# Four-layer attention kernel: in the fourth layer the softmax rows are scaled by ScalarE instead of VectorE, and the normed tokens are transposed as two ring jobs

## What is computed

```python
h = _mamba2_block(x, ...)                       # state-space scan over 112 steps, 8 heads of 64
xn = _ln(h, ln_w, ln_b)
q = (xn @ Wq).reshape(b, Lq, N_HEADS, dh)       # k = enc @ Wk, v = enc @ Wv the same way
scores = jnp.einsum('bqhd,bkhd->bhqk', q, k) * np.float32(1.0 / np.sqrt(dh))
scores = jnp.where(pad_mask[:, None, None, :], jnp.float32(-1000000000.0), scores)
p = jax.nn.softmax(scores, axis=-1)
ctx = jnp.einsum('bhqk,bkhd->bqhd', p, v).reshape(b, Lq, D)
return h + ctx @ Wo
```

## Time and profile before

| | |
|---|---|
| median of three runs | 3705.43 us (3703.78 to 3712.94) |
| profiled execution, its own time | 3712.93 us |
| its span in the trace | 3711.1 us |
| TensorE, VectorE, ScalarE, GpSimd busy | 93%, 52%, 50%, 11% |
| mean granted TensorE clock | 0.966 of full speed |
| fourth layer's attention and state turns | 3169 to 3711 us of the span |

### The profile page before, as it was taken

How to read it: one execution, slowest core, us unless ns; L and a number is a source line. 1 busy time by engine, 2 the same in 40 slices (tenths; PEclk the granted TensorE clock), 3 DMA queues, 4 the chain that set the end, 5 groups by cost and what they waited for, 6 DMA issues and landing times. The chain is left out here.

```text
span 3711.1 us, 67817 instructions
## 1 busy us (share of the span) xinstructions
PE 3461.5 (93%) x21748; PEld 2540.5 (68%) x21748; DVE 1933.5 (52%) x5863; ACT 1853.4 (50%) x5421; POOL 404.5 (11%) x488
## 2 busy tenths in 40 slices
PE   8999999999988999999979999999999997888888
PEld 6778778778866666666656766667667664555665
DVE  3654644654544444444544544544554545566656
ACT  3543544544445555555545555545545552444444
POOL 2101101101101111111010000000000001112111
PEclk9999999999998999999989999999999997898999
DMA  6000000000004000000010000000000000000000
GB/s 204 4 12 15 4 12 15 4 12 15 4 21 131 14 13 13 13 8 5 13 53 8 9 8 15 9 8 15 8 8 14 9 3 14 22 16 13 13 26 5
DMA packets 58462, 75.11 MB, mean 20 GB/s; under 512 B 6752, under 2 KB 55584, under 8 KB 57024
## 3 DMA queue, kind: packets, MB, share of 16 engines
q1 hardware_dynamic: 58176, 71.45, 6.3%
HBM read 64.04 MB, written 7.40 MB: 19 GB/s over the span
## 5 line engine op out<-in xcount | busy, mean ns | idle before, releaser
L161 PE MATMUL l_bank<-l_xT,weights_of_layers_and 128*128 128x224 f32 x2816 | 622.0, 374 | 18.7 <-ACT l_xT L1137 8.0
L161 PEld LDWEIGHTS l_bank<-l_xT,weights_of_layers_and 128*128 128x128 f32 x2816 | 546.4, 201 | 65.6 <-ACT l_xT L1137 8.7
L387 ACT ACTIVATE l_pT<-l_bank 125x336 f32<-125x336 f32 (+2 forms) x736 | 347.0, 471 | 339.5 <-PE l_bank L319 329.2
L319 PEld LDWEIGHTS l_bank<-identity,l_p 112*125 112x125 f32 (+2 forms) x2336 | 334.8, 178 | 185.6 <-issue 98.1
L319 PE MATMUL l_bank<-identity,l_p 112*125 112x112 f32 (+2 forms) x2336 | 390.1, 279 | 22.8 <-DVE l_p L363 18.5
L404 ACT ACTIVATE l_p<-l_p,l_nm 112x375 f32<-112x375 f32 x384 | 233.4, 608 | 287.2 <-DVE l_nm L438 285.9
L161 PE MATMUL l_bank<-weights_of_layers_and,l_cT 128*125 128x256 f32 (+2 forms) x960 | 303.3, 454 | 11.4 <-DVE l_queries_or_hidden L1839 9.3
L161 PE MATMUL l_bank<-l_cT,weights_of_layers_and 128*128 128x375 f32 x832 | 305.6, 497 | 0.0
L704 POOL TENSOR_TENSOR l_ve<-l_mv,eps 112x2 f32<-112x2 f32 (+1 forms) x89 | 17.3, 195 | 2434.7 <-DVE l_mv L698 2434.7
L363 DVE TENSOR_SCALAR l_p<-l_p,l_rs 112x375 f32<-112x375 f32 (+1 forms) x608 | 256.4, 422 | 21.7
L400 ACT ACTIVATE l_p<-l_p,l_nm 112x112 f32<-112x112 f32 x512 | 192.2, 377 | 150.7 <-DVE l_nm L434 131.9
(11 more groups left out here) (252 smaller groups left out, 5790.3 us busy)
## 6 DMA issues: line engine op xcount, KB each, us to landing
l_cT<-in_ctx_turned SPq DMA_DIRECT2D x32, 375.0 KB, 3.5
l_cx<-in_ctx SPq DMA_DIRECT2D x16, 375.0 KB
context_rows<-in_ctx_reversed SPq DMA_DIRECT2D x16, 375.0 KB
tokens<-x_after_layer SPq DMA_DIRECT2D x25, 224.0 KB, 2.6
x_after_layer<-l_z SPq DMA_DIRECT2D x24, 224.0 KB, 2.4
weights_of_layers_and<-bias_lines_kept SPq DMA_DIRECT2D x1, 2625.0 KB, 16.2
weights_of_layers_and<-in_L_xattn_w_fused SPq DMA_DIRECT2D x1, 2048.0 KB, 10.9
weights_of_layers_and<-in_L_xattn_w_ff SPq DMA_DIRECT2D x1, 2048.0 KB, 12.9
```

Source lines behind the costliest of these rows:

```text
L161: last = pe.matmul(out, left, right, start=(k == 0), stop=(k == len(pairs) - 1))
L319: last = pe.transpose(TR.bank(m)[:ph.keys, g * ph.rows:(g + 1) * ph.rows], p[:ph.rows, m % self.p_slots, g * ph.keys:(g + 1) * ph.keys], i ...
L387: return act.activation(out, src, ACT.Copy)
```

## The change

1. The cross attention's `Part` gets `scaled_by="act"`. The multiplication of an item's probabilities by the reciprocal moves from VectorE (a tensor_scalar) to ScalarE (an activation Copy whose scale is the column `rs`), in place as before. On ScalarE it stands in step n for item n-1, behind the exponential of item n. VectorE keeps the reciprocal. 128 instructions move. The other layers' parts keep their engines.
2. The job `yT` becomes two jobs, `yT0` and `yT1`, of 224 columns each in a bank of its own. ScalarE copies each as soon as it is there. `cq` waits for `yT1`. The ring's list has 33 jobs now.

```diff
3678.60:3711.10 32.50, Columns.scale
+        if ph.scaled_by == "act":
+            eng.activation(own, own, ACT.Copy, scale=self.rs[:r, c:c + 1]).then_inc(self.scaled["act"].sem, 1)
+        elif ph.n == 1 and ph.scaled_by == "dve":
-        if ph.n == 1 and ph.scaled_by == "dve":
             eng.tensor_scalar(own, own, self.rs[:r, c:c + 1], None, ALU.mult).then_inc(self.scaled["dve"].sem, 1)
3678.60:3711.10 32.50, Columns.scalar
-        self.lagged(parts, [(0, amid), (self.lag_t, turned), (0, exps), (self.lag_v, outputs)], between, amid)
+        def scaled(ph, k):
+            if ph.scaled_by == "act":
+                self.scale(act, i, ph, k)
+
+        self.lagged(parts, [(0, amid), (self.lag_t, turned), (0, exps), (1, scaled), (self.lag_v, outputs)], between, amid)
3678.60:3711.10 32.50, layer3
-                     sides=4, emptied_by="act")
+                     sides=4, emptied_by="act", scaled_by="act")
...
-                      19: [("cv10", "act"), ("yT", "act")], LAST: [("cv11", "act"), ("cq", "act")]}
+                      19: [("cv10", "act"), ("yT0", "act"), ("yT1", "act")], LAST: [("cv11", "act"), ("cq", "act")]}
3678.60:3711.10 32.50, layer3, TensorE
-                    turn_tokens(pe, c, P, i, "yT", xhat, normed.this(1))
+                    for t in range(KT):
+                        for sem, count in P.free(i, f"yT{t}", normed.this(1)):
+                            pe.wait_ge(sem, count)
+                        for j in range(PAIR):
+                            last = pe.transpose(P.bank(f"yT{t}")[:, j * T:(j + 1) * T], xhat[:, j, t * 128:(t + 1) * 128], c.ident[:T, :T])
+                        last.then_inc(P.full.sem, 1)
...
-                    project(pe, P, i, "cq", [columns(V["wq"], t) for t in range(KT)], xT, P.got("yT"))
+                    project(pe, P, i, "cq", [columns(V["wq"], t) for t in range(KT)], xT, P.got("yT1"))
3678.60:3711.10 32.50, layer3, ScalarE
-                    act.wait_ge(P.full.sem, P.count_full(i, "yT"))
                     for t in range(KT):
-                        last = act.activation(xT[:, t, :], P.bank("yT")[:, t * TP:(t + 1) * TP], ACT.Identity, scale=c.column["L3_ca_ln_w"][:, t:t + 1],
-                                              bias=c.column["L3_ca_ln_b"][:, t:t + 1])
-                    last.then_inc(P.emptier("yT").sem, 1)
+                        act.wait_ge(P.full.sem, P.count_full(i, f"yT{t}"))
+                        act.activation(xT[:, t, :], P.bank(f"yT{t}")[:, 0:TP], ACT.Identity, scale=c.column["L3_ca_ln_w"][:, t:t + 1],
+                                       bias=c.column["L3_ca_ln_b"][:, t:t + 1]).then_inc(P.emptier(f"yT{t}").sem, 1)
```

## The result

The changed kernel takes 3671.24 us (median of 5 runs, 3670.1 to 3673.39), the kernel before 3705.43 us (median of 5, 3703.78 to 3712.94): a ratio of 0.9897, 95% interval 0.9886 to 0.9908. The forecast was 3685 us. The direction is right, but the gain is 34 us where 20 were forecast. The profiled execution took 3673.39 us with a span of 3671.6 us, so 39.5 us less than the profiled one before.

What follows compares the result with a forecast made beforehand. VectorE's queue was taken to bound steps 2 to 9 of the long turns. 7 x (2.0 + 0.7) + 5.4 + 2.2 - 5.9 = 20.6 us gave a median of 3685 us (profiled 3692); range 3669 to 3700 us, the forecast's own 3678 to 3693.

Steps and rivals of the forecast that it cites:

- The next instruction starts 0.33 us after it: VectorE's queue, steps 2 to 9: seven multiplications at 0.33 us and one at 0.73 us, 3.0 us a turn gained.
- The two deductions of the middle: Steps 2 to 9: 0.2 us lost waiting for scores in step 3, 0.8 us to GpSimd's spreads; 2.0 us a turn remain.
- The taps against the spreads: VectorE's convolution taps of step 5 meet both GpSimd spreads, the engines holding each other up: 0.8 us lost, up to 2.0.
- Steps 10 and 11 are bound by TensorE, so the gain neither grows nor is lost there.: Long turns, behind VectorE's queue: the gain of steps 2 to 9 passes through unchanged, 0 us added.
- the first rival: Long turns: shorter waits in steps 8 and 9 raise the clock, 1.5 us a turn, 11 us more, 3674 us; chance 0.19.
- The end, 0.28 us a turn: End of each turn: copying the first half during the second's transposes saves the 0.28 us wait of cq, 2.2 us over eight.
- Steps 12 and 16: Long turns: TensorE's waits shrink by 0.33 us in step 12 and 0.37 us in step 16, together 0.7 us, ends 0 and 1.0.
- The last turn: Attention alone: the two-step ring grows from 2.46 to 3.18 us, 5.1 us over 14 steps, plus 0.8 at the end: 5.9 lost.
- The multiplication on ScalarE: ScalarE: one multiplication takes 0.61 us, from the exponential's row, and 0.5 us to the next instruction.
- The head: Start of a long turn: transposes no longer wait for ScalarE's query copies; 0.77 us gained, seven times 5.4 us.
- the move gives nothing: Rival: waits for ScalarE replace those for VectorE, leaving 7.6 us of ring jobs less 5.9 us: 3703 us; chance 0.12.
- Slower, by the clock: Rival: step 6 waits grow by over 1 us from 4.0, TensorE's clock stays low longer: 3718 us or more; chance 0.06.

Runs made afterwards that it cites:

- experiment 8: The changed kernel, but items 6 and 7 of each turn are multiplied by VectorE as before; 3682.58 us, ratio 0.993.
- experiment 9: The changed kernel with GpSimd's second spread cut to one element per head, leaving the second sequence's decays out; 3656.98 us, ratio 0.9863.
- experiment 7: The changed kernel with ScalarE's decays (dec) ahead of its multiplication of item 3 in step 4 of the long turns; 3670.85 us, ratio 0.9902.
- experiment 4: The kernel before, with two products of constants on TensorE ahead of its wait for the first spread in step 6; 3708.13 us, ratio 0.9991.
- experiment 6: The changed kernel with two products of constants on TensorE ahead of its wait for silu in step 9; 3667.44 us, ratio 0.9882.
- experiment 5: The changed kernel with two products of constants on TensorE ahead of its wait for GpSimd's first spread; 3669.58 us, ratio 0.9893.

## Why the prediction was wrong in size

Two steps of the prediction failed. It put the stretch behind VectorE's queue, steps 10 and 11, at nothing, and the clock made it 1.68 us a turn. And it priced a multiplication in VectorE's queue at 0.33 us, where it is 0.46 us. The path was right elsewhere: VectorE's queue sets steps 2 to 9, the head gains by the bank, the last turn loses. The sum was 20.6 us; the profiles differ by 39.5. By its own steps:

*"The next instruction starts 0.33 us after it"* (the price of a multiplication) was too low. I measured from the multiplication's start to the next start, and did not look one row up. Before, the reciprocal in front of it started 0.2 us earlier, because the multiplication waits for its result, and that gap belonged to the multiplication as well. The price is 0.46 us, shown by experiment 8. Over the middle it makes 8 x 0.13 = 1.0 us a turn more, and the same 0.13 us stands in step 12 (0.46 for 0.33).

*The two deductions of the middle* were 0.2 and 0.8 us. What VectorE won in step 2 was lost whole, 0.46 us: it waits 0.53 us for the next scores. The taps lost 3.69 - 3.08 = 0.61 us. The sum of the deductions was right, 1.07 against 1.0 us, and so the middle is 3.04 us by the higher price alone: 7.3 us over seven turns.

*The taps against the spreads.* The prediction let the two engines hold each other up. In the changed kernel it is almost all one-sided: both spreads ran at nearly their undisturbed pace (1.87 us each, where the shortest of the earlier trace rows took 1.79), and the taps paid the rest:

```profile
L2706 POOL TENSOR_TENSOR weights_of_layers_and<-l_dec,l_unit x16: 1825/1875/2902, 3125.2 to 3587.2; 112x896 f32<-112x896 f32 x16
```

The two spreads took 3.71 us together and ended at 3325.30 us. The six taps began at 3323.32 us, and the second of them stood until the spread had ended: 1.43 us, by experiment 9. The Trainium skill's "SBUF — State Buffer", section "SBUF: two separate sides", has the engine that starts first keep the pair of ports for its whole instruction while the other stands. The traces agree that one side stands whole: the one tap of 1.87 us, and in the other direction the spread. By the recorded starts they do not agree on who is first. Before, the first spread has its start at 3263.09 us, 0.12 us ahead of the three taps of step 4 (3263.21 us). Still the taps kept their 1.17 us, and the spread took 2.83 us. From the spread's recorded start to the end of those taps it is 1.29 us in that turn, 0.83 us in experiment 7 and 0.33 us in the changed kernel, and the spread grew by 1.04, 0.58 and 0.08 us: each time by 0.25 us less. So a spread behaves as if it took the ports some 0.25 us behind its recorded start, an estimate from these three. The taps before, then the first spread in experiment 7 and in the changed kernel:

```profile
3263.21 1.17 DVE L3022 SCALAR_TENSOR_TENSOR weights_of_layers_and<-weights_of_layers_and,conv_w 128x224 f32<-128x224 f32 x3
...
3317.84 2.37 POOL L2708 TENSOR_TENSOR weights_of_layers_and<-l_dec,l_unit 112x896 f32<-112x896 f32 x1 [14.60 <-ACT l_dec L2938]
...
3321.59 1.87 POOL L2706 TENSOR_TENSOR weights_of_layers_and<-l_dec,l_unit 112x896 f32<-112x896 f32 x1 [15.10 <-ACT l_dec L2952]
```

The three taps of step 4 start at 3317.50 us in experiment 7 and at 3320.75 us in the changed kernel and take 1.17 us in both.

*"Steps 10 and 11 are bound by TensorE, so the gain neither grows nor is lost there."* This step failed by 1.68 us a turn, 11.8 us in all by this turn against that one. The same products run there at a higher clock, 1.00 in the turn compared. It was the first rival, with 0.19, at 1.5 us a turn. With 20.6 + 11 us the rival gave 3681 us for the profiled execution; 3673.39 was measured, so it was the nearer of the two, and short by the middle's price. But it was not right by its own reason. It counted on TensorE standing still about 2 us less in steps 8 and 9. The waits there went from 1.08 + 1.59 + 1.29 = 4.0 us to 2.27 + 0.52 + 1.13 + 0.83 = 4.8 us: the rival did not foresee the new wait for item 5, 2.27 us. What spoke against the rival, that the waits of step 6 stay, had no bearing: experiments 4 and 6 show that a fall in step 6 costs nothing. Experiment 6 shows that TensorE's standing still in step 9 has a hand in the fall that does cost, since products in that place prevent it in all turns. Why the move alone spared the fall in four turns of seven, and made it shorter than the worst ones before, stays open.

The 11.8 us are also partly luck of the profiled executions, as said below the table of the parts. By the medians the forecast missed 34.2 - 20.4 = 13.8 us; without the 7.8 us of the other terms that leaves about 6 us for the clock, an estimate. Which of the two failed steps is the larger is therefore not settled.

*The end, 0.28 us a turn,* gave 0.02. The wait of `cq` is gone, but with 33 jobs in the ring `cv11` takes a bank that ScalarE empties later, and waits 0.30 us for it. The forecast followed `xT`, `b0` and `b1` to their new banks and not `cv11`. That the shift of banks causes the wait is read from its releaser; no kernel changed the bank alone. 2.2 us less than forecast.

*Steps 12 and 16:* 1.0 us together where 0.7 were taken and 1.0 was the upper end; 2.1 us more.

*The last turn:* 5.1 us lost, forecast 5.9. The ring over two steps took 3.25 us (3638.84 to 3642.09) where 3.18 were worked out. 14 steps at 0.36 us are 5.0 us, and at the 0.39 us of this ring 5.5 us, so the steps alone make up the 5.1 us. The 0.8 us that I added for the last item did not come.

```profile
3638.84 0.55 DVE L444 CUSTOM_DVE_ANT_0 l_p<-l_bank,l_padded 112x375 f32<-112x375 f32 x1
...
3639.53 0.59 ACT L406 ACTIVATE l_p<-l_p,l_nm 112x375 f32<-112x375 f32 x1
...
3640.12 0.59 ACT L363 ACTIVATE l_p<-l_p,l_rs 112x375 f32<-112x375 f32 x1
...
3640.86 0.55 PE L319 MATMUL l_bank<-identity,l_p 112*125 112x112 f32 x3
```

*The multiplication on ScalarE* takes 0.593 us where 0.61 was taken from the exponential's row. The Trainium skill's "ScalarE: Activation LUTs", section "What ACT_TABLE_LOAD costs", gives 280 ns + 0.833 ns an element for an activation with one column operand, an estimate of 592 ns for 375 elements. The trace agrees to 1 ns.

*The head:* 0.74 us against 0.77, and the new wait of 1.10 us before the scores that was named.

Together: 11.8 (clock) + 7.3 (middle) + 2.1 (steps 12 and 16) - 0.2 (head) - 2.2 (end) + 0.8 (last turn) = 19.6 us. With the forecast's 20.6 that is 40.2 us, beside the 40.5 us by which the fourth layer is shorter.

Of the rivals, "the move gives nothing" had a point: two new or longer waits for ScalarE did appear, 2.29 and 2.27 us. They cost nothing as far as the rows tell: TensorE waits for VectorE's own work behind each of them, and in experiment 7 one grew by 0.11 us and no turn changed. "Slower, by the clock" named its condition, the waits of step 6 longer by over 1 us together; they fell, from 4.0 to 3.1 us.

## What to carry to other kernels

The price of an instruction in a full queue is not its own step but the time from the instruction ahead of it to the one behind it, before and after: a dependent instruction also holds the gap in which it waits for its predecessor's result. Read a clock fall together with who is the bound while it lasts: under another engine's queue it was free here, and where TensorE is the bound, behind the queue or at the head of a turn, it cost 1.67 us each time. So look for a wait just ahead of such a stretch that can be filled. And a move that helps where two blocks overlap should be undone where one runs alone.

## What was not expected of the hardware

Two products of constants, 1.67 us of TensorE's time laid mostly into a wait that was there anyway, kept the granted clock at 1.00 in the 6 us that followed in all seven turns, where three of seven had lost it without them, at 1.67 us each; the same two products 10 us earlier changed nothing (experiments 5 and 6). And a spread on GpSimd made one of VectorE's six taps take 1.87 in place of 0.44 us while it lost 0.08 us itself and the other five taps nothing. With the taps ahead, three of them cost the spread 1.04 us and lost nothing.
